# Linear attention and product-key feed-forward on one core: the attention's second product laid in four column tiles, and a third head's mask on ScalarE

## What is computed

```python
qp = relu(einsum('bhsd,hdf->bhsf', q, rw)) + EPS      # 16 heads of DK=16, F=64 features each
kp = relu(einsum('bhsd,hdf->bhsf', k, rw)) + EPS
kv = einsum('bhsf,bhsd->bhfd', kp, v)
qkv = einsum('bhsf,bhfd->bhsd', qp, kv)               # the second product
norm = einsum('bhsf,bhf->bhs', qp, kp.sum(axis=2))
x = layernorm(x + (qkv / (norm + EPS)) @ Wo + bo)
# feed-forward: the best 8 of 64 x 64 products of two softmax-like scores per head (4 heads)
# pick experts among 1024; beside it a dense gated MLP
w = silu(x . down_embed[idx]) * softmax(scores)
x = layernorm(x + silu(x@Wg+bg)*(x@Wu+bu)@Wd + bd + w . up_embed[idx])
```

## Time and profile before

| what | value |
|---|---|
| median of 3 runs | 3634.39 us |
| the profiled execution | 3635.19 us |
| its span | 3633.4 us |
| granted TensorE clock, mean | 0.991 |
| TensorE busy | 3549.2 us, 98% |
| VectorE busy | 2585.7 us, 71% |
| ScalarE busy | 1981.3 us, 55% |
| GpSimd busy | 1514.3 us, 42% |

### The profile page before, as it was taken

One profiled execution on the slowest core, in us unless ns is written; L12 is line 12 of the kernel. 1 busy time (PEld: TensorE's weight loads), 2 busy tenths in 40 slices (PEclk: granted clock), 3 DMA queues, 4 the chain that ended last, 5 costly groups with the idle time before them and its releaser, 6 DMA issues.

```text
span 3633.4 us, 52250 instructions
## 1 busy us (share of the span) xinstructions
PE 3549.2 (98%) x19420; PEld 2929.1 (81%) x19420; DVE 2585.7 (71%) x5554; ACT 1981.3 (55%) x2886; POOL 1514.3 (42%) x1012
## 2 busy tenths in 40 slices
PE   8789999999999999999999999999999999999988
PEld 6668888888888888888888888888888888888877
DVE  4577777777777777777777777777677777777773
ACT  4455465555555555556555555555655554555551
POOL 0354344443344434444433444443444434555440
PEclk9899999999999999999999999999999999999999
DMA  3000000000000000000000000000000000000000
GB/s 118 18 12 18 13 13 12 18 18 12 12 18 12 18 18 13 12 18 13 18 18 13 13 13 18 18 14 17 13 12 18 18 7 12 13 13 12 7 6 12
DMA packets 23339, 61.17 MB, mean 17 GB/s; under 512 B 5552, under 2 KB 10032, under 8 KB 23088
## 3 DMA queue, kind: packets, MB, share of 16 engines
q1 hardware_dynamic: 18480, 41.04, 3.6%
q0 software_dynamic: 4608, 16.78, 1.1%
HBM read 41.04 MB, written 16.78 MB: 16 GB/s over the span
## 4 chain that ended last, share of the span: by engine, by line
PE 90%; DVE 3%; ACT 3%; POOL 1%; issue 1%; SPq 0%; DMA 0%; DVEq 0%; ACTq 0%; POOLq 0%
PE ring L639 28%; PE y_bank L732 12%; PE y_bank L734 11%; PE step_bank L554 6%; PE step_bank L562 6%; PE step_bank L666 6%; PE step_bank L639 5%; PE step_bank L598 3%; PE step_bank L656 3%; PE step_bank L548 3%; PE step_bank L590 3%; PE step_bank L712 3%; PE y_bank L728 1%; POOL grid L461 1%; DVE prob L1120 1%
## 5 line engine op out<-in xcount | busy, mean ns | idle before, releaser
L461 POOL TENSOR_TENSOR grid<-ex 128x1024 f32<-128x1024 f32 x512 | 1066.3, 2090 | 999.2 <-DVE prob L1117 364.3
L732 PE MATMUL y_bank<-wd_sb,gate 128*128 128x256 f32 x2048 | 621.6, 385 | 0.0
L734 PE MATMUL y_bank<-up_sb,wexp 128*128 128x256 f32 x2048 | 609.1, 379 | 0.0
L1107 DVE SCALAR_TENSOR_TENSOR grid<-grid,best 128x1024 f32<-128x1024 f32 x256 | 329.0, 1285 | 328.2 <-POOL grid L461 327.3
L1120 DVE SCALAR_TENSOR_TENSOR prob<-grid,narrow,prob 128x1024 f32<-128x1024 f32 x256 | 450.7, 1760 | 7.9
L639 PE MATMUL ring<-x1T_hl,downT_hl 128*128 128x512 f32 x1536 | 421.3, 409 | 17.2 <-ACT gate L883 17.2
L639 PE MATMUL ring<-x1T_hl,wg_hl 128*128 128x512 f32 x1536 | 428.8, 414 | 3.1 <-DVE gate L1136 3.1
L734 PEld LDWEIGHTS y_bank<-up_sb,wexp 128*128 128x128 f32 x2048 | 389.1, 190 | 52.8
L639 PE MATMUL ring<-x1T_hl,wu_hl 128*128 128x512 f32 x1536 | 422.2, 410 | 0.0
L732 PEld LDWEIGHTS y_bank<-wd_sb,gate 128*128 128x128 f32 x2048 | 354.0, 190 | 50.8 <-issue 22.7
L883 ACT ACTIVATE gate<-ring,bg_sb 128x512 f32<-128x512 f32 x256 | 176.3, 689 | 396.7 <-PE ring L639 395.0
(11 more groups left out here) (159 smaller groups left out, 5920.9 us busy)
## 6 DMA issues: line engine op xcount, KB each, us to landing
xb<-in_L_attn_x SPq DMA_DIRECT2D x34, 512.0 KB, 3.7
out_y<-x POOLq DMA_DIRECT2D x32, 512.0 KB, 3.0
xa<-in_L_attn_x SPq DMA_DIRECT2D x30, 512.0 KB, 3.7
prob<-in_L_ffn_down_embed SPq DMA_DIRECT2D x1, 1024.0 KB, 5.8
prob<-in_L_ffn_Wg SPq DMA_DIRECT2D x1, 1024.0 KB, 8.6
prob<-in_L_ffn_Wu SPq DMA_DIRECT2D x1, 1024.0 KB, 10.5
wd_sb<-in_L_ffn_Wd SPq DMA_DIRECT2D x1, 1024.0 KB, 11.4
up_sb<-in_L_ffn_up_embed SPq DMA_DIRECT2D x1, 1024.0 KB, 12.1
```

Source lines behind the costliest of these rows:

```text
L461: pool.tensor_tensor(grid[:, h % 2], bcast(ex[:, h, 0:NX].unsqueeze(2), [P, NX, NK]), bcast(ex[:, RH + h, 0:NK].unsqueeze(1), [P, NX, NK]) ...
L732: pe.matmul(rows, gate[:, c % 2, t * P:(t + 1) * P], wd_sb[:, c, :], start=(c == 0 and t % 2 == 0), stop=False, skip_group_check=True)
L734: mm = pe.matmul(rows, wexp[:, c % 2, t * P:(t + 1) * P], up_sb[:, c, :], start=False, stop=(c == C - 1), skip_group_check=True)
L1107: marks["keep", h] = rt_steps.mark(dve.scalar_tensor_tensor(out=g, in0=g, scalar=best[:, h, TOP - 1:TOP], in1=g, op0=ALU.is_ge, op1=ALU.mult))
```

## The change

- **Second product.** "qkv" and "back" go. For each half of the heads (j = 0, 1) there are "den" and "num": four matmuls each, whose stationary operand is 128x32 (`den_w` or `num_w` for two heads) and past which all 512 columns of `qp` stream. The four write partitions 0, 32, 64 and 96 of one bank, so the result is already transposed. `den_w` repeats the denominator over the 16 columns of a head.
- **Division.** ScalarE copies "den" into `attnT` (now in `x1`), adding a constant. VectorE's "divide" takes the reciprocal of 128x512 in place, and one operation adds a constant to "num" and multiplies. Both come in chunks 3 and 5, ahead of `ff_wexp` and the heads' additions.
- **EPS.** GpSimd's additions on `qp` go. Constants for EPS are formed once in a batch by a new step "consts" (16 matmuls of one column, two operations on VectorE). The bias of v moves out of the keys' part: a product with Wo, once at the start, puts it into `bo`.
- **Masks.** Three heads are masked by ScalarE; `keep` 2 goes from VectorE, and add 2 becomes a plain sum that stands after `keep` 3. In an odd chunk ScalarE does mask 1 and mask 2 in a row.
- **Queues.** The sum of attention and x stays in `xb`, so the next load of `xb` waits for the norm instead of "wo". The store of the output moves from GpSimd's queue to SyncE's.

The parts of the diff stand in this order: the order of the steps, SyncE, TensorE (once at the start, once in a batch, then the attention's steps), ScalarE, VectorE.

```diff
-    AT_SEQ = ([("turn", 0), ("turn", 1), ("q", 0), ("q", 1)] + [("qp", j) for j in range(4)] + [("qkv", 0)]
-              + [("qp", 4), ("qp", 5), ("qkv", 1), ("qp", 6), ("qp", 7), ("qkv", 2), ("qkv", 3)]
-              + [("back", 0), ("back", 1), ("wo", 0), ("wo", 1), ("next", 0), ("next", 1)])
+    AT_SEQ = ([[("turn", 0)], [("turn", 1)], [("q", 0)], [("q", 1)]] + [[("qp", j)] for j in range(4)] + [[]]
+              + [[("den", 0), ("num", 0)], [("divide", 0), ("qp", 4)]] + [[("qp", j)] for j in range(5, 8)] + [[]]
+              + [[("den", 1), ("num", 1)], [("divide", 1)], [], [("wo", 0)], [("wo", 1)], []])
...
-        RT_TILE = ["top", "less", "cand", "best", "sum", "rz", ("keep", 2), ("add", 1),
-                   ("add", 2), ("keep", 3), ("add", 3), "mass"]
+        RT_TILE = ["top", "less", "cand", "best", "sum", "rz", ("add", 1), ("keep", 3), ("add", 2),
+                   ("add", 3), "mass"]
...
-                        sp.wait_ge(*drained("at", m - 1, "wo", 1))
+                        sp.wait_ge(x1_ready, m * T)
                     sp.dma_start(xb[:], x_groups[m]).then_inc(xb_loaded, 16)
+                if last:
+                    sp.wait_ge(y_ready, (f + 1) * T)
+                    sp.dma_start(out_groups[f], y_sb[:]).then_inc(y_stored, 16)
...
+            for k in range(KD):
+                mm = pe.matmul(ring[0][:, 0:D], bv_sb[:, k:k + 1].broadcast_to([P, P]), wo_sb[:, k, :],
+                               start=(k == 0), stop=(k == KD - 1))
...
+            def consts_use(a):
...
+                for col, kind in enumerate(("num", "den")):
+                    for c in range(FC):
+                        row, at = 2 * DK * (c % 4), 2 * col + c // 4
+                        mm = pe.matmul(bank[row:row + 2 * DK, at:at + 1], weights(kind, c), neg_half[:, 0:1],
+                                       start=True, stop=True)
...
-                        for t in range(T):
-                            for c in range(2):
-                                mm = pe.matmul(at_bank[:, (2 * t + c) * W:(2 * t + c + 1) * W],
-                                               qp[:, (2 * j + c) % 4, t * P:(t + 1) * P],
-                                               kv_blocks[:, 2 * j + c].rearrange("p a b -> p (a b)"),
-                                               start=True, stop=True)
-                    elif kind == "back":
-                        pe.wait_ge(*drained("at", m, "qkv", 2 * j + 1))
-                        mm = turn(at_bank, x1, j)
...
+                        for k in range(4):
+                            mm = pe.matmul(at_bank[2 * DK * k:2 * DK * (k + 1), :], weights(kind, 4 * j + k),
+                                           qp[:, k, :], start=True, stop=True)
                     elif kind == "wo":
-                        pe.wait_ge(*drained("at", m, "back", 1))
+                        pe.wait_ge(*drained("at", m, "num", 0))
+                        pe.wait_ge(*drained("at", m, "num", 1))
...
+                    elif kind == "den":
+                        if last and j == 0:
+                            act.wait_ge(y_stored, (it - LAST_LAG + 1) * 16)
+                        act.wait_ge(*drained("kv", batch * BG - 1, "consts", 0))
+                        read_by(act.activation(attnT[:, j, :], at_bank[:], ACT.Identity,
+                                               bias=consts[:, 2 + j:3 + j]), "at", m, kind, j)
...
                     if rt and c % 2:
-                        mask(c // 2, 1)
+                        mask(c // 2, 1), mask(c // 2, 2)
...
+                    elif kind == "divide":
+                        rows = attnT[:, j, :]
+                        dve.wait_ge(*drained("at", m, "den", j))
+                        at_steps.mark(dve.reciprocal(rows, rows))
                         at_steps.wait()
...
+                        read_by(dve.scalar_tensor_tensor(out=rows, in0=bank_of("at", m, "num", j)[:],
+                                                         scalar=consts[:, j:j + 1], in1=rows, op0=ALU.add,
+                                                         op1=ALU.mult), "at", m, "num", j)
...
-                        keep(t, 2)
...
-                        add_head(t, 1), add_head(t, 2)
+                        add_head(t, 1)
...
-                        add_head(t, 3), clamp(t)
+                        add_head(t, 2), add_head(t, 3), clamp(t)
```

More of the change, by code:

```diff
@@ L48, in block_kernel @@
     BG = S // G
-    ACT_HEADS, STEEP = 2, float(2 ** 30)
+    ACT_HEADS, STEEP = 3, float(2 ** 30)
     ATTN_EPS, LN_EPS = 1e-6, 1e-5
@@ L108, in block_kernel @@
         xbT = qp[:, 2:4]
-        den = sb("den", P, T, 4)
-        attnT = xbT
+        consts = sb("consts", P, 4)
         x1 = sb("x1", P, T, D)
+        attnT = x1[:].rearrange("p t d -> p (t d)").rearrange("p (h n) -> p h n", h=2)
         stats, mv1, rstd1 = sb("stats", P, T, 6), sb("mv1", P, T, 2), sb("rstd1", P, T)
@@ L177, in block_kernel @@
         Y_STEPS = 2 * T
[L180 to L183, removed]
+        AT_EARLY, AT_MID, AT_LATE = ([AT_SEQ[3 * c + k] for c in range(C - 1)] for k in range(3))
+        AT_EARLY.append([]), AT_MID.append([]), AT_LATE.append([("next", 0), ("next", 1)])
         kv_places = [(c, place) for c in range(C) for place in range(3) if place or c >= C - 2]
@@ L187, in block_kernel @@
         assert len(kv_places) == KV_USES
[L190 to L193, removed]
+        WORK = {"turn": 0.44, "k": 1.73, "q": 1.73, "v": 1.73, "kp": 0.47, "qp": 0.46, "den": 0.95, "num": 0.95, "consts": 0.6, "sum": 1.73,
+                "wo": 1.73, "next": 0.44, "rt": 1.39, "pt": 0.44, "fold": 2.6, "ff": 1.39, "out": 1.73}
+        HOLD = {"turn": 2.0, "k": 6.0, "q": 6.0, "v": 4.0, "kp": 2.0, "qp": 2.0, "den": 2.0, "num": 8.0, "consts": 2.0, "sum": 3.0,
+                "wo": 3.0, "next": 5.0, "rt": 8.0, "pt": 5.0, "fold": 9.0}
         place, taken = {}, [0] * (STEP_BANKS + 2)
@@ L219, in block_kernel @@
                                           ("kv", it - 1, [("fold", 0)] if c == 0 and it <= NG and it % BG == 0 else []),
+                                          ("kv", it - 1, [("consts", 0)] if c == 1 and it <= NG and it % BG == 0 else []),
                                           ("pt", it - FFN_LAG, [(c,)] if ff else []), ("out", 1, []),
@@ L226, in block_kernel @@
                     for use in uses:
-                        take(name, group, *use)
+                        if use[0] != "divide":
+                            take(name, group, *use)
         def bank_of(*use):
@@ L643, in at_use @@
                 def at_use(kind, j):
+                    if kind == "divide":
+                        return
                     at_bank = bank_of("at", m, kind, j)
@@ L840, in at_use @@
                 def at_use(kind, j):
-                    if kind in ("qkv", "wo"):
+                    if kind in ("num", "divide", "wo"):
                         return
@@ L1017, in blocks, with constants @@
                 read_by(ins, "kv", (b + 1) * BG - 1, "fold", 0)
+            def constants(b):
+                a = (b + 1) * BG - 1
+                bank = bank_of("kv", a, "consts", 0)
+                dve.wait_ge(*full("kv", a, "consts", 0))
+                dve.scalar_tensor_tensor(out=consts[:, 0:2], in0=bank[:, 0:2], scalar=-2 * ATTN_EPS, in1=bv_eps[:],
+                                         op0=ALU.mult, op1=ALU.add).then_inc(consts_ready, 1)
+                read_by(dve.tensor_scalar(consts[:, 2:4], bank[:, 2:4], -2 * ATTN_EPS, ATTN_EPS, ALU.mult, ALU.add),
+                        "kv", a, "consts", 0)
             def body(it, par, kv, at, rt, ff, last, batch):
@@ L1167, in uses @@
                             kv_use(a, *use)
-                        if use[0] in ("q", "qkv", "wo", "next") and at:
+                        if use[0] in ("q", "divide", "wo", "next") and at:
                             at_use(*use)
```

120 lines of the change are left out of this document (56 added, 64 removed).

## The result

| what | before | after |
|---|---|---|
| median | 3633.84 us (4 runs, 3632.43 to 3635.32) | 3525.11 us (4 runs, 3522.2 to 3527.5) |
| ratio, 95% interval | | 0.970 (0.9684 to 0.9717) |
| span of the profiled execution | 3633.4 us | 3522.2 us |
| granted TensorE clock, mean | 0.991 | 0.991 |

The account below looks back on a forecast made before the run. TensorE, busy 98% of the span, was taken as the bound: -113 us from its shorter steps, +10 "consts", +1 bias, +8 ScalarE stalls, sum -94, giving 3540 us; range for 8 in 10, 3508 to 3585.

Parts of the forecast that it names:

- two at a time: Rival on TensorE: only two of four column tiles run together, "den" and "num" 3.87 us, kernel 3651 us; chance 0.05.
- the records keep their order: Rival on TensorE: records start strictly in turn, "den" and "num" 4.30 us, kernel 3677 us; chance 0.05.
- ScalarE gives out: Rival: mask 2 waits for its spread at chunk 2, 1 to 2 us an iteration, kernel 3562 to 3592; chance 0.15.
- The steady part: Iterations 6 to 31, TensorE full: the forecast's sum laid over them gave -83.5 us.
- Change of mode: TensorE getting in and out of column tiles: 0.43 us, paid once for each "den" and "num" pair.
- "consts": TensorE, once in a batch: 16 small matmuls at 1.3 us, times eight, +10 us; bounds 4 and 17.
- ScalarE's stall: Between chunks 1 and 2, mask 2 against the gate's silu: 0.3 us an iteration, +8 us in all, between 0 and 45.
- The first iterations: Iterations 4 and 5, no feed-forward to cover latencies: counted at nothing, between -8 and +13 us.
- Iterations 32 to 36: Iterations with no more keys: the forecast's sum laid over them gave -12.7 us.
- The end: Iterations 37, 38 and the end: forecast 0; the store issued by SyncE was to bring nothing, within 1 us.
- The divide: VectorE, chunks 3 and 5: 4.1 us each, covered by idle time before `keep` 2 and before "wo", stall of nothing.
- The rule on efficiency: Alternative size from the Trainium skill: column tiles at 2.38 times for three, a step 1.09 us, kernel about 3568 us.

Follow-up runs that it names:

- experiments 6 and 7: Changed kernel with each "den" and "num" matmul cut into two of 256 columns, a tile's two in a row or tiles in turn: 3524.65 and 3524.88 us.
- experiment 4: Changed kernel with mask 2 moved to the end of the chunk on ScalarE, behind its AT_LATE steps: 3503.50 us.
- Experiment 10: The kernel of experiment 4 with the step "consts" one chunk later, in chunk 2 instead of chunk 1: 3496.02 us.
- experiment 9: Kernel before the change with only the third head's mask moved to ScalarE, placed last in its chunk: 3625.88 us.
- experiment 3: Changed kernel with the reciprocal replaced by a cheap operation of the same shape, leaving the division out: 3520.88 us.
- Experiments 2 and 5: Changed kernel with the third mask back on VectorE: divide behind `keep` 2 (experiment 2) 3665.81 us, divide ahead of it (experiment 5) 3517.25 us.

## Why the prediction was right, and where it was off

**The mechanism stood.** TensorE is full, and what leaves its order of work comes off the iteration. Tiles on separate partitions run side by side at full rate: 16 records in four rounds of 0.43. Both rivals on the tiles fall, "two at a time" by the 1.85 us, "the records keep their order" by experiments 6 and 7. "ScalarE gives out" was right in its place, chunk 2, but neither in its cause (mask 2 does not wait for its spread; a relu waits behind mask 2) nor in its size: 17 us there, not 30 to 60.

**The steady part was right by luck.** Over iterations 6 to 31 some 23 us of gain that the forecast lacked stand against 23 of loss that it lacked:
- *Change of mode*, a term that was mis-sized: 0.43 was taken, 0.33 measured. The 0.09 at the entry was already inside the 1.00 of "sum" on the chain, and I added it again. 2 x 0.1 x 26 makes 5 us more gain.
- *The neighbours of the steps.* Plain iterations without the new wait (experiment 4) take 104.53 us against 108.94, so 4.41 less, where the pieces on the chain give 8.08 - 4.10 = 3.98. From start to start, "qkv" and "back" took 7.60, "den" and "num" take 3.71, and all other steps together are 0.51 shorter. I had priced one "qkv" and one "back" and had looked at a neighbour of the "qkv" alone. That is 0.43 an iteration, 11 us more gain.
- *"consts"*: 1.3 us was taken, and it is 0.4 from start to start, 0.6 with its neighbours: 4 us more gain in six batches. A record of one column is far shorter than one of 128; the bound below was nearer.
- *The bank round*: no term at all. "consts" takes a bank, and all later steps of the iteration get another one than before. The wait is listed with 10.9 us. Where the clock doesn't fall, an iteration with a fold is now 5.6 us longer than a plain one without ScalarE's wait, and was 3.0 longer before; less "consts" that leaves 2.1 each, 12 to 13 us lost. Experiment 10 takes the listed wait away and gets back 6 of them.
- *ScalarE's stall*: 0.27 us an iteration was taken. Measured are 0.56 by the list and 0.85 from start to start (experiment 4), in 20 iterations: 10 us more loss, and at another wait. I followed the gate's silu and had not looked at what else stands behind mask 2 in ScalarE's queue: a relu that empties a bank.
- The granted clock falls in four of these six batches where it was five before (below): 1.7 us more gain. The mask gives 0.9 in iteration 6 (experiment 9).

Together they come to 1 us of gain against the forecast, and the table has 0.9.

**The ends were under-counted**, and this is the part that failed by most.
- *The first iterations*, counted at nothing (-8 to +13): 8 of gain against 5.5 of exposed reciprocal (experiment 3), 1.4 reckoned for bias and "consts" and 1.5 of gain by the mask (experiment 9) would be -2.6; -1.0 was measured.
- *Iterations 32 to 36* gained 20.0 us instead of 12.7. In 33 to 35 it is 4.2 to 4.6 each where 3.5 was forecast: without keys there is no projection of v to stall, and a group gives 4.41, not 3.78. Iteration 32 gained 6.1 instead of 2.2: no stall, a cheaper "consts", and no fall of the clock behind its fold, as there was before. The 0.9 in iteration 36 is the mask's.
- *The end* gained 5.9 us. In experiment 9 the mask gives 2.2 there. Some 3 are the store: from its issue by GpSimd to the end of the span it took 6.0 us before (3627.36 to 3633.4), from SyncE 3.1 us (3519.14 to 3522.2). I had said "nothing, within 1 us". The transfer itself lands 2.9 and 2.6 us after its issue, so most of the difference lies between the landing and the end of the span. It is 6.0 us in the three traces whose store stands on GpSimd's queue and 3.0 in the nine others; why is open, and no run moved the store alone.

The forecast had costed the mask where TensorE is full, and nowhere else.

**The divide** cost nothing, as forecast, but the reason given was luckier than it was good. "The divide falls into that hole" is true only since the change also takes away `keep` 2, for whose spread the hole was a wait. Experiments 2 and 5 show what hung on it: some 145 us. The forecast named a price (60 us for each microsecond in each divide) but gave this case no chance.

**The rule on efficiency.** The Trainium skill (TensorE: Matmul & The Clock Gate, Measured speedup vs the span model) gives 2.38 times for three column tiles; a factor like that was estimated to make a step 1.09 us and the time 3568. The trace does not agree: four rounds of 0.43 fill 1.72 of the 1.85 us, and what is lost is 0.33 us at a change of mode. "sum", half as long, loses as much (1.00 + 0.20 - 0.86 = 0.34), so the loss goes by the change and not by the work. The Trainium skill also says on that page (The mechanism) that matmuls start and end in program order; across column tiles experiments 6 and 7 don't bear that out.

## What to carry to other kernels

On an engine that works in order, a long operation belongs ahead of one that waits: behind it, it holds a PSUM bank for the length of the wait, and a full TensorE stops for the bank. Two parts that each lose alone (+26 and +30 us) can gain 109 together, and here one line of order gave as much without the second part; so before a second part is credited, ask which wait it took away and whether an order would do. Where TensorE was full here, load on the others counted only at the hand-over of a bank, so each queue is to be read for every reader of a bank, not for the one wait that looks tight. What a step or a wait costs is read from start to start, neighbours included: the pieces of the chain missed 0.43 us of 4.41, and a wait listed with 0.56 cost 0.85. What the ends of the run gain has to be counted by itself.

## What was not expected of the hardware

**The granted clock dips inside a full TensorE.** In the kernel before, behind a fold (two matmuls of 256 columns, then eight of 33), with TensorE busy throughout. Windows of 1 us, columns as in the earlier trace rows:

```profile
1770.00:1771.00 1.00, 1.00 (x5) 0.80 (x4) 0.54 (x1) 0.29 (x1) 0.02 (x1) 0.50 0.00 0
1771.00:1772.00 1.00, 1.00 (x2) 0.34 (x1) 0.00 (x0) 0.39 (x2) 0.00 (x0) 0.50 0.55 61
1772.00:1773.00 1.00, 1.00 (x2) 0.34 (x1) 0.00 (x0) 0.00 (x0) 0.00 (x0) 0.50 0.79 307
1773.00:1774.00 1.00, 1.00 (x5) 0.64 (x4) 0.00 (x0) 0.32 (x1) 0.00 (x0) 0.96 0.39 156
```

The clock is 0.50, its 1.2 GHz level, for the projection that follows the fold's small matmuls. Iterations with a fold in the kernel after take 111.8 us where the clock falls and 110.1 where it doesn't, so one fall costs 1.7 us. From the fold of iteration 8 on it falls in six of seven batches before, and in four of seven after, there mostly some 18 us behind the fold, past "consts" and the new wait. What decides it was not tried.

**A reciprocal costs by the element**, some 6.2 ns for each more (178 ns for 4, 3342 for 512), nearly five times the 0.7 us of other operations of that width.

**VectorE and GpSimd get in each other's way.** In experiment 2 the addition at 1936.40 takes 3.03 us while GpSimd spreads a head (1936.45, 1.90 us), against 1.28 for its like alone. In the kernel before it is one or the other in all 128 places where an addition and a spread start within 0.1 us of each other: 66 times the addition takes 3.0 and the spread 1.9, and 62 times the addition takes 1.28 and the spread 3.0. So one of the two pays for most of the other; what decides which is not known.
